# Two-layer window and causal attention on one core: three waits at the change of layers and in the last image are rearranged

## What is computed

```python
x = x + L0(gn(x))   # 8x8 windows shifted by 4, 16 heads of 16, cosine attention, bias, softmax
x = x + L1(gn(x))   # pairs of images are one batch of 512 tokens; heads as below
return x
```

```python
s = einsum('bhqe,bhke->bhqk', q, k) * scale
mask = i[:, None] <= i[None, :] if lookahead else i[:, None] >= i[None, :]
p = softmax(where(mask, s, finfo.min))          # 8 heads look back, 8 look ahead
o = einsum('bhqk,bhke->bhqe', p, v);  out = concat(o) @ Wo.T
```

## Time and profile before

| | us |
|---|---|
| median of 3 runs | 1207.15 |
| lowest, highest | 1199.74, 1212.03 |
| profiled execution | 1203.1 |
| its span | 1201.4 |
| layer zero's last output starts | 536.68 |
| first full burst of layer one | 548.34 |
| last image's first scores | 1154.72 |
| last image's stores | 1178.39 |

### The profile page before, as it was taken

One profiled execution on the slowest core, in us unless ns is written; L12 is line 12 of the kernel. 1 busy time (PEld: TensorE's weight loads), 2 busy tenths in 40 slices (PEclk: granted clock), 3 DMA queues, 4 the chain that ended last, 5 costly groups with the idle time before them and its releaser, 6 DMA issues.

```text
span 1201.4 us, 50875 instructions
## 1 busy us (share of the span) xinstructions
PE 1148.9 (96%) x21406; PEld 839.9 (70%) x21406; DVE 947.5 (79%) x1704; ACT 639.4 (53%) x1051; POOL 209.2 (17%) x271
## 2 busy tenths in 40 slices
PE   6899999999999999998999999999999999999983
PEld 3677777777777777776767777777777777777752
DVE  5588888888888888865688787878787787878753
ACT  4456566666666666543555555555555555555530
POOL 1001111111111111111121221212222212222120
PEclk9799999999999999998999999999999999999977
DMA  2100000000000000000122312222222223132222
GB/s 86 58 24 21 16 17 20 19 19 18 17 17 17 17 10 3 4 3 1 29 60 51 71 39 67 43 63 45 62 45 61 56 50 69 40 68 42 64 46 71
DMA packets 180189, 46.04 MB, mean 38 GB/s; under 512 B 146308, under 2 KB 179350, under 8 KB 180118
## 3 DMA queue, kind: packets, MB, share of 16 engines
q1 hardware_dynamic: 178056, 43.76, 15.7%
q10 hardware_dynamic: 2064, 1.26, 0.4%
HBM read 27.56 MB, written 17.30 MB: 37 GB/s over the span
## 4 chain that ended last, share of the span: by engine, by line
PE 85%; DVE 7%; issue 4%; ACT 1%; DMA 1%; SPq 1%; POOL 0%; ACTq 0%; POOLq 0%; DVEq 0%
PE psG L1087 14%; PE psA L491 10%; PE psA L1129 8%; PE psG L1109 6%; PE psA L1148 5%; PE psA L430 5%; PE psE L444 5%; PE psE L1187 5%; PE psA L1162 4%; PE psG L387 4%; PE psG L411 3%; DVE stack L1392 3%; PE psE L465 3%; PE psA L455 3%; DVE stack L1387 2%
## 5 line engine op out<-in xcount | busy, mean ns | idle before, releaser
L1361 DVE TENSOR_REDUCE cm<-psG 128x4 f32<-128x1024 f32 (+1 forms) x192 | 235.0, 1224 | 120.1 <-PE psG L1109 120.0
L1233 ACT ACTIVATE probs<-psG 128x1024 f32<-128x1024 f32 x192 | 196.6, 1024 | 146.6 <-PE psG L1087 146.3
L1087 PE MATMUL psG<-stack 32*128 32x256 f32 (+1 forms) x2048 | 222.9, 346 | 11.2 <-DVE cm L1361 8.0
L1439 POOL TENSOR_SCALAR_AFFINE_SELECT probs<-probs 128x1024 f32<-128x1024 f32 x128 | 139.6, 1102 | 495.3 <-ACT probs L1233 495.3
L1096 PE MATMUL psG<-stack 32*128 32x256 f32 (+1 forms) x2048 | 220.6, 342 | 0.9 <-issue 0.9
L1087 PEld LDWEIGHTS psG<-stack 32*128 32x128 f32 x2048 | 152.9, 188 | 69.7 <-DVE cm L1361 27.6
L1096 PEld LDWEIGHTS psG<-stack 32*128 32x128 f32 x2048 | 150.1, 185 | 3.3 <-issue 3.0
L894 POOL TENSOR_TENSOR X<-X,probs 128x96 f32 (+5 forms) x128 | 64.3, 533 | 471.0 <-ACT probs L622 471.0
L491 PE MATMUL psA<-probs,xh 128*128 128x512 f32 x256 | 128.5, 627 | 2.2 <-ACT xh L655 1.6
L1387 DVE RECIPROCAL stack<-stack 128x128 f32<-128x128 f32 x128 | 115.7, 929 | 10.0 <-DMA stack<-totals 10.0
L1148 PE MATMUL psA<-xh,wqk 128*128 128x256 f32 x512 | 122.7, 383 | 0.0
(11 more groups left out here) (145 smaller groups left out, 1891.3 us busy)
## 6 DMA issues: line engine op xcount, KB each, us to landing
X<-in_xr SPq DMA_DIRECT2D x32, 256.0 KB, 2.7
scratch_heads<-stack SPq DMA_DIRECT2D x128, 64.0 KB
stack<-scratch_heads SPq DMA_DIRECT2D x32, 256.0 KB
stack<-totals SPq DMA_DIRECT2D x64, 128.0 KB
out<-X SPq DMA_DIRECT2D x32, 256.0 KB, 3.1
totals<-stack SPq DMA_DIRECT2D x128, 4.0 KB
probs<-in_wqk ACTq DMA_DIRECT2D x1, 512.0 KB, 4.4
wqk<-in_wqk SPq DMA_DIRECT2D x1, 512.0 KB, 3.9
```

The source lines that it names most:

```text
L1087: last = nc.tensor.matmul(G[:, to:to + b.size], km[i.k][own_rows(r), o, e, b.keys_of(o) * P:(b.keys_of(o) + 1) * P], qm[i.k][own_rows(r), ...
L1233: nc.scalar.activation(weights[i.k][:, b.weights_at:b.weights_at + 1024], G[:, 0:1024], ACT.Exp).then_inc(exp_done, 1)
L1361: nc.vector.reduce_max(slots, scores, AX_X).then_inc(max_done, 1)
L1439: nc.gpsimd.affine_select(out=diagonal, in_=diagonal, compare_op=ALU.is_ge, fill=0.0, base=0, pattern=[[0, QUADS], [0, 2], [sign, P]], cha ...
```

## The change

Layer zero's last output on TensorE goes behind layer one's opening bursts, and on ScalarE the copy of layer one's first values ahead of the output's copy. In layer one's last image the bursts with a B put their scores into banks 2 and 3, and each burst waits for the exponential two bursts back. The last image's eight stores are issued on ScalarE's queue. Layer one's output(29) goes from behind WHOLE_1 to behind weigh(30, 1).

```diff
-            pipeline(pe, images, [(scores, 0), (project_v, 1), (only(LAST, bounds_begin), -1), (output, -1), (only(LAST, bounds_end), -1), (bounds, 1), ...
+            pipeline(pe, images, [(scores, 0), (project_v, 1), (only(LAST, bounds_begin), -1), (only(LAST, bounds_end), -1), (output, -1), (bounds, 1), ...
...
-                                   (copy_v, 1), (copy_z, -1), (normalize, 3), (copy_qk, 2), (bias_across, 1),
+                                   (copy_v, 1), (only(LAST, later.copy_v), -1), (copy_z, -1), (normalize, 3), (copy_qk, 2), (bias_across, 1),
...
+def scores_bank(i, b, images):
+
+    return 2 if here(i, images - 1) and b.at % 2 else 0
...
         def regroup(i):
-
+            if here(i, images - 1):
+                return
...
-                wait(pe, exp_done, i.count(ALL, b.at) if b.at else i.plus(-1).count(ALL))
+                if here(i, images - 1) and b.at:
+                    wait(pe, exp_done, i.count(ALL, b.at - 1))
+                else:
+                    wait(pe, exp_done, i.count(ALL, b.at) if b.at else i.plus(-1).count(ALL))
...
-                            to = bank * 512 + b.column(o, e)
+                            to = (scores_bank(i, b, images) + bank) * 512 + b.column(o, e)
...
+        def output_in_turn(i):
+            if not here(i, images - 3):
+                output(i)
+
+        def output_late():
+            output(Image(0, images - 3))
...
                                   B(HALVES), (lambda i: weigh(i, 1), -1),
+                                      (only(images - 1, output_late), -1),
                                   B(HALVES_B), (lambda i: project_qk(i, 0), 2),
-                                  B(WHOLE_1), (lambda i: turn_c(i, 0), 1), (output, -2),
+                                  B(WHOLE_1), (lambda i: turn_c(i, 0), 1), (output_in_turn, -2),
...
+        def regroup_last():
+            i = Image(0, images - 1)
+            act.wait_ge(ot_out[0], images)
+            act.wait_ge(ot_out[1], images)
+            act.wait_ge(loaded[i.k], i.plus(-2).dmas(LOADS))
+            for c in range(QUADS):
+                act.dma_start(scratch[i.k].rearrange("m e (g c j) -> e c g m j", g=QUADS, c=QUADS)[:, c],
+                              ots[COL * c:COL * c + DIM, :, :].rearrange("e g (m j) -> e g m j", j=DIM)
+                              ).then_inc(stored[i.k], 16)
+            for g in range(QUADS):
+                act.dma_start(totals[i.k].rearrange("m (g c j) -> g c m j", g=QUADS, c=QUADS)[g],
+                              ots[DIM:P:COL, g, :].rearrange("c (m j) -> c m j", j=DIM)).then_inc(stored[i.k], 16)
...
-            nc.scalar.activation(weights[i.k][:, b.weights_at:b.weights_at + 1024], G[:, 0:1024], ACT.Exp).then_inc(exp_done, 1)
+            base = scores_bank(i, b, images) * 512
+            nc.scalar.activation(weights[i.k][:, b.weights_at:b.weights_at + 1024], G[:, base:base + 1024],
+                                 ACT.Exp).then_inc(exp_done, 1)
...
                                    X_(HALVES), (lambda i: copy_outputs(i, 1), -1),
+                                       (only(images - 1, regroup_last), -1), (copy_v, 1), X_(HALVES_B), (copy_q, 2),
```

More of the change, by code:

```diff
@@ L528, in bounds_end @@
                 later.burst(WHOLE_1B)
-            pipeline(pe, images, [(scores, 0), (project_v, 1), (only(LAST, bounds_begin), -1), (output, -1), (only(LAST, bounds_end), -1), (bounds, 1), (turn, 2), (only(LAST - 1, later.project_first), 0),
+            pipeline(pe, images, [(scores, 0), (project_v, 1), (only(LAST, bounds_begin), -1), (only(LAST, bounds_end), -1), (output, -1), (bounds, 1), (turn, 2), (only(LAST - 1, later.project_first), 0),
                                   (only(LAST, later.project_second), 0), (table_read, 0), (sums, 0), (weigh, 0), (only(LAST, lambda: later.burst(WHOLE_0)), 0),
@@ L658, in _ @@
             pipeline(act, images, [(lambda i: exponent(i, 0), 0), (lambda i: exponent(i, 1), 0), (only(LAST, later.keys), 0),
-                                   (copy_v, 1), (copy_z, -1), (normalize, 3), (copy_qk, 2), (bias_across, 1),
+                                   (copy_v, 1), (only(LAST, later.copy_v), -1), (copy_z, -1), (normalize, 3), (copy_qk, 2), (bias_across, 1),
                                    (only(LAST - 1, later.queries_keys), 0),
-                                   (only(LAST, later.second_queries_keys), 0), (copy_o, 0), (lambda i: square(i, 0), 3), (lambda i: square(i, 1), 3), (bias_within, 1), (copy_c, 1), (only(LAST, later.copy_v), -1)], LAGS, once={-3: rectify_early, -2: rectify_late, -1: open_table})
+                                   (only(LAST, later.second_queries_keys), 0), (copy_o, 0), (lambda i: square(i, 0), 3), (lambda i: square(i, 1), 3), (bias_within, 1), (copy_c, 1)], LAGS, once={-3: rectify_early, -2: rectify_late, -1: open_table})
             later.rest()
@@ L1275, in rest @@
             pipeline(act, images, [(lambda i: copy_outputs(i, 0), -1), X_(WHOLE_0), (lambda i: copy_k(i, 1), 1), X_(WHOLE_0B),
-                                   X_(HALVES), (lambda i: copy_outputs(i, 1), -1), (copy_v, 1), X_(HALVES_B), (copy_q, 2),
+                                   X_(HALVES), (lambda i: copy_outputs(i, 1), -1),
+                                       (only(images - 1, regroup_last), -1), (copy_v, 1), X_(HALVES_B), (copy_q, 2),
                                    X_(WHOLE_1), (lambda i: copy_k(i, 0), 2), X_(WHOLE_1B)], LAGS, start=0)
```

## The result

| | before | after |
|---|---|---|
| median, us | 1205.32 (20 runs, 1199.03 to 1219.81) | 1194.41 (20 runs, 1191.15 to 1209.15) |
| profiled execution's span | 1201.4 | 1195.1 |

The ratio is 0.9927, with a 95% interval from 0.9903 to 0.9951: 8.8 us less, between 5.9 and 11.7. It leaves out the runs more than 1.5% above the fastest of their kernel and is not the quotient of the two medians, which differ by 10.9 us. The forecast was 7.8 us less, a median of 1199.4 within 1190.3 to 1207.2.

The account below looks back on a forecast made before the run. TensorE carries 85% of the chain that ended last, so edits pay where it idles or runs slowly and in the last microseconds. 2.4 + 5.4 + 0 = 7.8 us off the 1207.15 median gives 1199.4, range 1190.3 to 1207.2.

Parts of the forecast that it names:

- The opening bursts: Change of layers: layer zero's last output behind WHOLE_1B fills TensorE's 1.57 us stall; a new 1.5 us wait follows; gain 2.4 us.
- the half-speed stretch that doesn't come: Change of layers: TensorE's second-image projections run at full speed, not 3.56 us; nearly all of the 2.4 us gain.
- the first stall only changes its name: Rival at the change of layers: without half speed before, gain there is 0, 5.4 us in all, 1201.7; chance 0.18.
- Its sum of 5.4 us: Whole gain in the rival with no gain at the change of layers: 5.4 us in all, so 1201.7.
- Scores in both bank pairs: Last image: WHOLE_0B and HALVES no longer wait for the preceding exponential; weigh(30, 1) starts at 1158.4 instead of 1161.29.
- The older output: Last image: output(29) waits 1.65 us for image 29's division ahead of HALVES_B; with a clock fall, WHOLE_1B comes 5.4 us earlier.
- 6.95 us and not 5.4: WHOLE_1B's gain in the last image: 6.95 us if the clock holds in output(29)'s wait, 5.4 if it falls.
- From WHOLE_1B to the end: Tail: 5.7 us to the copy as before, image 30's stores in by 1167.8, ahead of need; stores start at 1173.0.
- a sign of being wrong: Tail: the prediction is wrong if the last image's eight stores take longer than 7.1 us to arrive.
- Stores on ScalarE's queue: Last image's eight issues change queue and save nothing: bounds 0.7 us gained or as much lost, taken as 0.
- the prediction's bound of 1 us: Tail: overlap of the stores with image 30's fetch would make the sum up to 1 us less.
- The sum: Whole kernel: 2.4 + 5.4 + 0 = 7.8 us gained, taken off the median 1207.15: 1199.4; remaining chance 0.42.

Follow-up runs that it names:

- the second profile of before: The kernel before, unchanged, profiled once more: ratio 0.9997 to the kernel before, layer stage 615.9 us, end 45.5 us behind the last image's first scores.
- the part alone: Kernel before with only the opening's edits on TensorE and ScalarE: ratio 0.9992 to the kernel before, median 1201.71 or 1201.68 us.
- the run with the banks alone: Kernel before with only the last image's scores in two bank pairs and their wait: ratio 0.9952 to the kernel before, end 40.1 us behind first scores.
- the run with that order: Changed kernel with output(29) behind weigh(30, 1) and ahead of HALVES_B: ratio 0.9986, end 41.8 us behind the last image's first scores.

## Why the prediction came out, step by step

**The opening bursts, 2.4 us.** The mechanism was right in each step: projection and HALVES follow at once, the residual is late next, a new wait of 1.5 us (1.80 measured) with VectorE as its releaser. The size came out in the pair of profiles (618.9 to 616.2). It was not the change that took the stretch away, though: the second profile of before has 615.9 without it, the part alone gave 0.9992, and in two of eight profiles the clock fell behind the new wait instead. What is left open is whether the new order makes the fall rarer. The step that failed is the sentence that nearly all of it is "the half-speed stretch that doesn't come", priced in full, as if that stretch came each time. The prediction's own rival ("the first stall only changes its name", chance 0.18) described this. Its sum of 5.4 us failed with the other step.

**Scores in both bank pairs.** HALVES at full speed behind WHOLE_0B, weigh(30, 1) behind it without a gap: at 1159.30, 3.4 us behind the first scores, where 3.7 were worked out. Right, and the run with the banks alone shows that it carries the tail.

**The older output.** The step that failed: wrong place. The prediction had 1.65 us of waiting and 3.5 us of output on the path, and took the clock to fall there. None of it exists. Put where the prediction had it, it comes close: 1.88 us of waiting, 3.10 of output, WHOLE_1B at 12.6. One reading in that step is wrong as well. A wait of 1.65 us leaves 2.35 us of work in 4, not 2.2, and that is the 2.36 of the window in which the clock held; by this comparison the prediction would have had 6.95 us and not 5.4. In the same 4 us of the run with that order the wait was longer, the work 2.12 us, and the clock fell, so the choice came out right by luck. In the change WHOLE_1B came 5.5 us earlier than forecast (7.1 against 12.6).

**From WHOLE_1B to the end.** "As before" failed as a result of it. The prediction had stated its condition, that image 30's stores must be in before the copy, and had them at 1167.8, 13.1 us behind the first scores (13.25 measured). With WHOLE_1B 5.5 us earlier that was no longer ahead of need, and the stores started at 14.5, not at 12.8. The eight stores then took 9.6 us and not 7.1, which the prediction had named as a sign of being wrong.

**Stores on ScalarE's queue, 0.** Right in sum, 39.2 with either queue. The overlap cost 2.1 us, so the prediction's bound of 1 us was too small. The trace agrees with what the prediction took from the Trainium skill (DMA: Bandwidth & Descriptors, "Issuing engines are not separate DMA queues"), that transfers of all engines interleave.

**The sum.** 7.8 forecast, 8.8 measured, and in the tail 5.4 forecast and 6.3 to 7.5 by stages. Two errors nearly cancel: up to 2.4 us too much at the opening, and 1 to 2 too little in the tail. There 5.5 us more at WHOLE_1B left 2.1 at the end against the first profile: 1.7 went in the wait for the buffer and 2.5 in the transfers, and 0.8 came back between fetch and end. The 8.8 us of the ratio is more than the tail's 7.5 by stages, but the interval holds it; what the rest is, chance or clock, stays open. So the forecast was right in amount and in its main mechanism, the bank pairs. That its terms add up to the right sum is luck.

## What to carry to other kernels

Where a stall and a slow stretch stand together in a profile, price the stall at full clock and look whether a second profile shows the slow stretch at all; only what remains is the change's. Two bank pairs in turn for the last image, where nothing else uses the second, took out all but 0.62 us of three short waits and the 10 to 14 us at half speed that came with them, for a few lines. When an edit names an image and a lag, work out the step before placing it in the order.

## What the runs showed of the hardware

The same kernel with the same stall (1.57 and 1.56 us, 2.43 and 2.44 us of work in 4) had its clock fall to the 1.2 GHz level in one execution and keep 2.4 GHz in the other. In the last image it fell in both, 4.1 and 3.1 us behind the first scores, and stayed down 14 us in the one and twice, 7 and 4 us, in the other. So the share of work around a stall does not settle it alone, in these runs.

An issue is not a fixed cost on either queue. Of the last image's 64 KB stores one took 0.69 us and the one before it 3.15 on ScalarE's queue, with image 30's fetch and image 29's store in flight. On SyncE's queue, in the same place, the issues took 0.63 to 1.99 us; after image 30's fetch had landed, on ScalarE's, 0.68 to 1.28.
